# A graph, attention and expert layer on one core: last LayerNorm in two VectorE passes, first residual tiles read into used weight blocks

## What is computed

```python
x = x + gnn(xn, ...) + mix(xn[None], ...)[0]
x = x + ffn(_layernorm(x)[None], ...)[0]

# ffn, for its one batch entry; two of four experts are chosen by a router on the mean token
h = einsum('bld,edh->belh', x, w1) + b1          # 768 -> 1536 for each expert
h = act_i(h)                                     # gelu, silu, mish, gelu
out = einsum('belh,ehd->beld', h, w2) + b2       # 1536 -> 768
y = einsum('be,beld->bld', gate, out) + x        # x here: the normed input of the block
mu = y.mean(-1); var = ((y - mu) ** 2).mean(-1)
return (y - mu) * rsqrt(var + 1e-5) * ln_g + ln_b
```

## Time and profile before

| | us |
|---|---|
| median of three executions (lowest, highest) | 2075.46 (2067.35, 2075.83) |
| the profiled execution, its own time | 2072.92 |
| its span, from the first to the last instruction | 2071.2 |
| PE busy in the span | 1942.0 |
| DVE / ACT / POOL busy | 1173.4 / 624.5 / 434.0 |

### The profile page before, as it was taken

How to read it: one execution, slowest core, us unless ns; L and a number is a source line. 1 busy time by engine, 2 the same in 40 slices (tenths; PEclk the granted TensorE clock), 3 DMA queues, 4 the chain that set the end, 5 groups by cost and what they waited for, 6 DMA issues and landing times.

```text
span 2071.2 us, 28372 instructions
## 1 busy us (share of the span) xinstructions
PE 1942.0 (94%) x10999; PEld 1840.6 (89%) x10999; DVE 1173.4 (57%) x2091; ACT 624.5 (30%) x1218; POOL 434.0 (21%) x321
## 2 busy tenths in 40 slices
PE   6799897999988899999999999999989999999995
PEld 3476786999878899888899999999989999999995
DVE  8877446898687332667744352442467334274347
ACT  2541224888676231222510010010241001011024
POOL 1000002112000332503243141330205224043020
PEclk9899998999989899999999999999989999999998
DMA  4231311111123321003221120110222012021013
GB/s 136 96 120 66 101 44 40 40 54 47 65 80 112 120 62 39 24 1 117 86 61 31 31 62 8 54 54 8 61 89 79 23 39 62 9 76 46 16 40 125
DMA packets 76829, 125.50 MB, mean 61 GB/s; under 512 B 3346, under 2 KB 47418, under 8 KB 76701
## 3 DMA queue, kind: packets, MB, share of 16 engines
q1 hardware_dynamic: 76700, 123.77, 18.5%
HBM read 98.30 MB, written 25.45 MB: 60 GB/s over the span
## 4 chain that ended last, share of the span: by engine, by line
PE 76%; DVE 8%; DMA 5%; ACT 4%; issue 3%; SPq 2%; POOL 0%; DVEq 0%; ACTq 0%; POOLq 0%
PE pb L1001 24%; PE pa L619 24%; PE pb L619 11%; PE pa L771 3%; PE pb L909 2%; PE pa L758 2%; PE pb L771 2%; PE pa L672 2%; DMA md<-md_d 2%; DMA wt_d<-xu 2%; ACT sm L1374 1%; PE pb L802 1%; SPq L415 1%; DMA raw<-in_L_gnn_Wu 1%; DVE st L2022 1%
## 5 line engine op out<-in xcount | busy, mean ns | idle before, releaser
L1591 ACT ACTIVATE tr<-pb,V 128x418 f32<-128x418 f32 (+1 forms) x144 | 87.9, 610 | 770.0 <-PE pb L1001 770.0
L1001 PE MATMUL pb<-X_hi,uw_hi 128*128 128x416 f32 (+1 forms) x864 | 306.0, 354 | 3.2 <-DVE uw_lo L2129 3.2
L1001 PE MATMUL pb<-X_hi,uw_lo 128*128 128x416 f32 (+1 forms) x864 | 305.6, 354 | 0.0
L1001 PE MATMUL pb<-X_lo,uw_hi 128*128 128x416 f32 (+1 forms) x864 | 305.5, 354 | 0.0
L619 PE MATMUL pa<-dw_hi,hh 128*125 128x384 f32 x960 | 246.4, 338 | 0.7 <-ACT tr L1591 0.7
L619 PE MATMUL pa<-dw_hi,hl 128*125 128x384 f32 x960 | 246.0, 337 | 0.0
L619 PE MATMUL pa<-dw_lo,hh 128*125 128x384 f32 x960 | 245.9, 337 | 0.0
L2076 DVE CAST hh<-tr 128x418 fp32r<-128x418 f32 (+1 forms) x144 | 116.7, 811 | 209.2 <-ACT tr L1591 209.2
L1145 POOL CAST uw_hi<-raw 128x768 fp32r<-128x768 f32 x47 | 42.4, 901 | 699.7 <-PE pb L1001 608.6
L619 PEld LDWEIGHTS pa<-dw_hi,hh 128*125 128x125 f32 x960 | 172.4, 185 | 1.1 <-ACT tr L1591 1.0
L619 PEld LDWEIGHTS pa<-dw_hi,hl 128*125 128x125 f32 x960 | 172.9, 185 | 0.0
(11 more groups left out here) (383 smaller groups left out, 3603.6 us busy)
## 6 DMA issues: line engine op xcount, KB each, us to landing
raw<-in_L_mix_fc_w SPq DMA_DIRECT2D x48, 384.0 KB, 3.2
raw<-in_L_ffn_w SPq DMA_DIRECT2D x47, 384.0 KB, 3.2
md<-md_d SPq DMA_DIRECT2D x20, 610.4 KB
md_d<-mds SPq DMA_DIRECT2D x10, 610.4 KB
raw<-in_L_mix_qkv_w SPq DMA_DIRECT2D x24, 192.0 KB, 5.1
TOK<-in_x SPq DMA_DIRECT2D x10, 375.0 KB
xn_d<-TOK SPq DMA_DIRECT2D x10, 375.0 KB
xu<-in_x SPq DMA_DIRECT2D x10, 375.0 KB
```

Of the source, the lines that this page charges most:

```text
L1001: last = nc.tensor.matmul(pb[:, j % 4, 0:n], w_[:, kk, :], x_[:, kk, o:o + n], start=(kk == 0 and q == 0), stop=(kk == KT - 1 and q == 2))
L1591: last = A_(RE[f"tr{j % 3}"][:, 0:w], pb[:, j % 4, 0:w], ACT.Identity if func == "mish" else func, bias=bias(b))
```

## The change

Four things are changed, all of them in the last group and behind it.

1. **Loads of x2.** The first EARLY = 4 tiles of `x2` go to a new buffer `X2e` in area RE, over the weight buffers `uw` 0 and 1. SP issues loads 0 and 1 when the last group's up block b = 1 is done, loads 2 and 3 after block b = 2, and loads 4 to 9 where all ten were issued before. Tiles 4 to 9 lie in area RX as before.
2. **Offsets.** `x2 + ln_b` for tiles 0 to 3 is computed by DVE within the last group's `hidden`, behind jobs 9, 10 and 11 (one, one and two tiles). Tile t + 4 is done in tile t's turn of the last loop.
3. **The norm.** The last `down` also gives the row sum of what it writes (`accum_out`). DVE makes the negated mean of it. One pass then writes (y + (-mu)) * ln_g to a buffer `cen`; ACT computes the sum of squares and the root from `TK`, for all ten tiles; a second pass writes cen * (1/sd) + (x2 + ln_b) to the tile. ACT's row sum, ACT's mean and ACT's `normal` pass, and DVE's moments, `nm`, `gained` and the former `output` are gone. All steps of a tile stand in that tile's turn.
4. **The last store.** Tile 9 is finished and stored in two halves of 384 columns, the first from SP's queue, the second from ACT's.

```diff
-FACT = 8
+EARLY = 4
...
-                  [("X2", [TP, NT, D], fp32)])
+                  [("X2", [TP, NT - EARLY, D], fp32)] + [(f"cen{q}", [TP, D], fp32) for q in range(2)])
...
-                  + [("pre", [P, EXP, D], fp32)])
+                  + [("pre", [P, EXP, D], fp32)],
+                  [("X2e", [TP, EARLY, D], fp32), ("sq", [TP, D], fp32)])
...
+        X2 = [RE["X2e"][:, t, :] if t < EARLY else RX["X2"][:, t - EARLY, :] for t in range(NT)]
...
-            sp.wait_ge(*at("up_mm", JOBS * ALL_GROUPS))
             for t in range(NT):
-                sp.dma_start(RX["X2"][:, t, :], x2_d[t]).then_inc(sem(f"X2_in{t}"), 16)
-            for t in range(NT):
+                if t in (0, 2):
+                    sp.wait_ge(*at("up_mm", up_last(GK * ALL_GROUPS - 3 + t // 2)))
+                if t == EARLY:
+                    sp.wait_ge(*at("up_mm", JOBS * ALL_GROUPS))
+                sp.dma_start(X2[t], x2_d[t]).then_inc(sem(f"X2_in{t}"), 16)
+            for t in range(NT - 1):
                 sp.wait_ge(*at("f_o", t + 1))
                 sp.dma_start(out_t[t], TK[:, t, :]).then_inc(sem("f_out"), 16)
-            sp.wait_ge(*at("f_out", 16 * NT))
+            sp.wait_ge(*at("f_o", NT))
+            sp.dma_start(out_t[NT - 1][:, 0:HD2], TK[:, NT - 1, 0:HD2]).then_inc(sem("f_out"), 16)
+            sp.wait_ge(*at("f_out", 16 * (NT + 1)))
...
             def spread_of(t):
 
-                act.wait_ge(*at("dn_acc", NT * (ALL_GROUPS - 1) + t + 1))
-                A_(RE["x2s0"][:], TK[:, t, :], ACT.Copy, accum_out=st[:, t, 0, 0:1]).then_inc(sem("f_sum"), 1)
-                act.wait_ge(*at("f_sum", t + 1))
-                A_(mv[:, t, 0:1], st[:, t, 0, 0:1], ACT.Copy, scale=-1.0 / D).then_inc(sem("f_mean"), 1)
                 act.wait_ge(*at("f_mean", t + 1))
-                A_(RE["x2s1"][:], TK[:, t, :], ACT.Square, bias=mv[:, t, 0:1], accum_out=st[:, t, 0, 1:2]).then_inc(sem("f_sq"), 1)
+                A_(RE["sq"][:], TK[:, t, :], ACT.Square, bias=mv[:, t, 0:1], accum_out=st[:, t, 0, 1:2]).then_inc(sem("f_sq"), 1)
                 act.wait_ge(*at("f_sq", t + 1))
                 A_(ve[:, 3, t:t + 1], st[:, t, 0, 1:2], ACT.Sqrt, scale=1.0 / D, bias=eps["eps5"]).then_inc(sem("f_sd"), 1)
 
             for t in range(NT):
-                if t < FACT:
-                    spread_of(t)
-                else:
-                    root("f", t, "eps5", FACT)
-                if t >= 1:
-                    normal("f", t - 1, TK[:, t - 1, :], TK[:, t - 1, :])
-            normal("f", NT - 1, TK[:, NT - 1, :], TK[:, NT - 1, :])
+                spread_of(t)
+            act.wait_ge(*at("f_o", NT + 1))
+            act.dma_start(out_t[NT - 1][:, HD2:D], TK[:, NT - 1, HD2:D]).then_inc(sem("f_out"), 16)
...
+            def early_offsets(n):
+
+                if n == JOBS - 3:
+                    dve.wait_ge(*at("gb_in", 32))
+                for t in {JOBS - 3: (0,), JOBS - 2: (1,), JOBS - 1: (2, 3)}.get(n, ()):
+                    offset(t)
...
-            def gained(t):
-
-                dve.wait_ge(*at("f_xh", t + 1))
-                v.tensor_tensor(TK[:, t, :], TK[:, t, :], RW["b2r0"][:], ALU.mult).then_inc(sem("f_m"), 1)
...
+            def centred(t):
+
+                dve.wait_ge(*at("dn_acc", NT * (ALL_GROUPS - 1) + t + 1))
+                v.tensor_scalar(mv[:, t, 0:1], st[:, t, 0, 0:1], -1.0 / D, None, ALU.mult).then_inc(sem("f_mean"), 1)
+                dve.wait_ge(*at("f_mean", t + 1))
+                v.scalar_tensor_tensor(out=RX[f"cen{t % 2}"][:], in0=TK[:, t, :], scalar=mv[:, t, 0:1], in1=RW["b2r0"][:],
+                                       op0=ALU.add, op1=ALU.mult).then_inc(sem("f_cn"), 1)
+
+            def output(t, parts):
+
+                dve.wait_ge(*at("f_sd", t + 1))
+                v.reciprocal(rs[:, 0, t:t + 1], ve[:, 3, t:t + 1]).then_inc(sem("f_rc"), 1)
+                dve.wait_ge(*at("f_rc", t + 1))
+                dve.wait_ge(*at("f_cn", t + 1))
                 dve.wait_ge(*at("f_x2", t + 1))
-                v.tensor_tensor(TK[:, t, :], TK[:, t, :], X2[:, t, :], ALU.add).then_inc(sem("f_o"), 1)
...
+                for a, b in parts:
+                    v.scalar_tensor_tensor(out=TK[:, t, a:b], in0=RX[f"cen{t % 2}"][:, a:b], scalar=rs[:, 0, t:t + 1], in1=X2[t][:, a:b],
+                                           op0=ALU.mult, op1=ALU.add).then_inc(sem("f_o"), 1)
+
+            for t in range(NT):
+                dve.wait_ge(*at("dn_acc", NT * (ALL_GROUPS - 2) + t + 1))
+                down(ALL_GROUPS - 1, t, gate[0:TP, TOPK - 1:TOPK], accum_out=st[:, t, 0, 0:1])
+                centred(t)
+                if t + EARLY < NT:
+                    offset(t + EARLY)
+                output(t, ((0, D),) if t < NT - 1 else ((0, HD2), (HD2, D)))
```

More of the change, by code:

```diff
@@ L174, in gps_layer @@
                ("r_pool", 1), ("r_idx", 1), ("r_d", 1), ("r_gates", 1), ("f_last", 1))
-        follow("dve_rows", ("wt_ev", NT), ("g_ev", NT), ("h2_ev", NT), ("xg_ev", NT), ("kv_ev", 2 * NT), ("l_x1", NT), ("b2_add", 2 * NT), ("f_m", NT))
+        follow("dve_rows", ("wt_ev", NT), ("g_ev", NT), ("h2_ev", NT), ("xg_ev", NT), ("kv_ev", 2 * NT), ("l_x1", NT), ("b2_add", 2 * NT), ("f_cn", NT))
         for k in ("st", "ag", "rc", "sd", "rs", "xh"):
@@ L2079, in hidden, with down @@
                     hook(n)
-            def down(group, t, scale=None, out_=None):
+            def down(group, t, scale=None, out_=None, **kw):
                 d = NT * group + t
@@ L2089, in down @@
                 else:
-                    ins = v.scalar_tensor_tensor(out=w2(out_), in0=wide(pa, t % 2), scalar=scale, in1=w2(tok), op0=ALU.mult, op1=ALU.add)
+                    ins = v.scalar_tensor_tensor(out=w2(out_), in0=wide(pa, t % 2), scalar=scale, in1=w2(tok), op0=ALU.mult, op1=ALU.add, **kw)
                 ins.then_inc(sem("dn_acc"), 1)
@@ L2156, in out_bias, with offset @@
                 return add
+            def offset(t):
+                dve.wait_ge(*at(f"X2_in{t}", 16))
+                v.tensor_tensor(X2[t], X2[t], RW["b2r1"][:], ALU.add).then_inc(sem("f_x2"), 1)
+            def early_offsets(n):
[3 more added lines that the diff above has]
+                    offset(t)
             def expert(e, mish):
@@ L2160, in expert @@
                     grp = MLP_GROUPS + EXP_GROUPS * e + g
-                    hidden(grp, mish, out_bias(e) if g == 0 else lambda n: None)
+                    hidden(grp, mish, out_bias(e) if g == 0 else early_offsets if grp == ALL_GROUPS - 1 else lambda n: None)
                     if g < EXP_GROUPS - 1 or e < TOPK - 1:
@@ L2174, in _ @@
                     expert(e, None)
-            X2 = RX["X2"]
-            def gained(t):
-                dve.wait_ge(*at("f_xh", t + 1))
-                v.tensor_tensor(TK[:, t, :], TK[:, t, :], RW["b2r0"][:], ALU.mult).then_inc(sem("f_m"), 1)
[L2183 to L2189, removed]
-                dve.wait_ge(*at("f_x2", t + 1))
-                v.tensor_tensor(TK[:, t, :], TK[:, t, :], X2[:, t, :], ALU.add).then_inc(sem("f_o"), 1)
```

## The result

| | before | changed |
|---|---|---|
| median of five executions | 2075.46 us | 2061.20 us |
| ratio of the runs | 1 | 0.9948 (95% interval 0.9927 to 0.9969) |
| profiled execution, own time / span | 2072.92 / 2071.2 | 2060.88 / 2059.1 |

The change is faster by 0.5%, with an interval that excludes no change and reaches from 0.3 to 0.7%. One of its five executions, 2418.16 us at a granted clock of 0.745, is left out of the ratio. The forecast was 2062 us. The two medians lie 14.3 us apart and the ratio says some 11; later medians of the kernel before were 2071.4 to 2072.3 us, so the median of five overstates the gain.

The account below looks back on a forecast made before the run. The DMA queue was taken as the bound after 2008 us; 12.4 us less gave span 2058.8 and execution 2060.5, or 2063.1 with the median's 2.5 us offset; between them 2062 us was forecast, range 2054 to 2069.

Parts of the forecast that it names:

- The bound: After 2008 us: one DMA queue with 20 load and store tiles, 3.07 us each, sets the end at 2071.
- 16 x 3.07 us: DMA queue from 2009.6 us: four early loads leave 16 tiles, 49.1 us, ending at 2058.7, 12.4 us earlier.
- Early loads and offsets at 0: Last up phase: early loads find the queue empty and offset passes fit DVE's idle gaps, so both cost 0.
- A turn of 4.07 us: DVE's last loop: a tile's turn with an offset takes 4.07 us against PE's 4.20, so it just fits.
- the term of 0.87: DVE's turn: centred pass and output, each 0.87 us to the next start, taken from the 768-wide pass of 959 ns.
- The fit in 4.20: DVE's turn of 4.07 us must fit PE's 4.20 us a tile; the prediction said it just fits.
- rival B: DVE becomes the bound, its last turn about 4 us late: span 2062.8, time 2066 us; chance 0.13.
- After PE: Tile 9 on DVE after PE's last work: halves start at 2053.6 and 2054.1, DVE ends 6.8 us earlier than 2060.87.
- The last store: Tile 9's halves: 1.5 us from issue to packets, one after the other on five engines, 3.07 us together, landing at 2058.8.
- Its own sign of being wrong: End of the kernel: the prediction is wrong if the last landing comes more than 5 us behind DVE.
- Rival A: Last store: the two halves run side by side, 1.6 us more gain, 2060.5 us; chance 0.08.
- Rivals C and D: C: early loads do not shorten the queue, 2074 us, chance 0.04; D: PE stalls, its clock falls, 2087 us, chance 0.03.

Follow-up runs that it names:

- late_loads: Changed kernel with all ten x2 loads again behind the last up job, each offset in its own tile's turn; span 2070.5 us, ratio 0.9999.
- two_early: Changed kernel with two x2 loads early in place of four, each tile's offset two turns ahead; span 2060.4 us, ratio 0.9968.
- rows_late: Two-pass norm, loads and stores of the end cut as 112 + 13 rows, no early load or offset, against the changed kernel; span 2059.5 us, ratio 0.9947.
- early_only: Kernel before with only the four early loads and early offsets, its old norm kept; span 2068.5 us, ratio 0.9996.
- whole_store: Changed kernel with tile 9 finished in one pass and stored whole from SP; span 2059.6 us, ratio 0.9954.
- rows_before: Kernel before with each of the ten x2 loads and ten stores cut as 112 + 13 rows; span 2069.1 us, ratio 0.9968.

## Why the prediction was right, and where not

**The bound.** That the queue and not DVE or PE's end set 2071 is shown by late_loads: 5 us less on DVE, nothing on the span.

**16 x 3.07 us.** Right in size: the tail fell by 11.4 us for 12.4, and from the changed kernel to two_early to late_loads a tile costs 2.6 and 3.1 us. The condition "if every store is ready when its turn comes" carried more than the text gave it: without it the same loads are worth 0.2 us. It was met narrowly. The prediction had store 8 in time by 1.2 us. SP issued it 41.8 us behind the start of the down products, and by the small packets the five engines were done with store 7 at 43.4 to 44.2 (2050.7 to 2051.5 in the profile); with 1.5 us to the first packets that leaves between nothing and 0.9 us.

**Early loads and offsets at 0.** Right. The last up phase takes 41.03 us and the down phase 42.03, as before. The offsets' passes on DVE fit the gaps of the earlier trace rows, and rows_late shows a gain that I had not priced as one: 1.6 us of DVE's end.

**A turn of 4.07 us.** Measured 4.18. The accumulator's read was 0.08, as in the earlier trace rows. Mis-sized was the term of 0.87 for the centred pass and the output: 1.02 us long, 0.93 to the next start. The row to take was the down pass, which also has a scalar for each partition, and not the 959 ns. The fit in 4.20 had 0.02 us of room, not 0.13; rival B was nearer than its chance said.

**After PE.** DVE's end was put at 2054.1, 46.1 us behind the start of the down products; measured 46.1.

**The last store.** Here the sum came near by luck: two errors largely cancel. The step that failed is the latency: I took 1.5 us from the bytes of the queue's first 2 us (its first packets come 0.9 us behind the issue, some of them held for 0.9 us and more) and added one steady transfer. Stores without a backlog took 5.5 to 9.4 us from issue to landing in early_only, and 7.6 in whole_store. Against that, I gave the halves no gain, and they have 2 to 3 us. What is left is 1 us: 5.7 us from DVE's end to the end of the span where the prediction had 4.7. Its own sign of being wrong, a landing more than 5 us behind DVE, did appear: the last half landed at 2058.7, 5.3 us behind. Rival A (the halves side by side over two queues) is out: the small packets of SP's half end at 2056.0 and those of ACT's half at 2058.4, one after the other, and from one queue the tail is no longer. The Trainium skill (DMA: Bandwidth & Descriptors, "Why a DMA increments its semaphore by 16 and not by 1") has 16 engines for 112 rows and 13 for 13: the 29 small packets a tile of rows_before agree.

**Rivals C and D** did not occur: two_early and late_loads price the loads near the forecast, and PE's granted clock is 1.00 in every stretch shown up to 2050 us.

**The number.** That the median of 2061.20 lies 0.8 us from the forecast is luck too. The forecast stands between two sums 2.6 us apart, and the measured one starts its down products 0.7 us early.

## What to carry to other kernels

When two things end close to each other, price each alone before adding them: here the loads alone and the norm alone gave nothing, and together 0.5%. A DMA's share of the engines tells how many take part; 0.32 in a full queue points at the shape of its transfers, and with rows cut as 112 + 13 throughout the program the change won 1.8%, where it won 0.5% without. A profile of one kernel can start a late phase 5 us apart from another's: measure a change at the end from the last point that it cannot touch.

## What was not expected of the hardware

A 375 KB transfer of 125 rows has no single price. By the packets in the traces it takes 2.95 to 3.05 us in a backlog, but up to 9.4 us from issue to landing into an empty queue, with one of five engines last. Two such stores issued 1.9 us apart landed 4.3 us apart. Cut as 112 + 13 rows it kept SP waiting for 1.9 us behind its issue. Cutting it into smaller transfers on five engines, by rows or by columns, won 2 us. Why the engines hold single packets up to six times as long when no backlog stands ahead, and why one of them ends last, is open.
